# Gelu of the first three tiles from square, exponential and reciprocal on ACT and DVE

## The reference

```python
def _L1_attn_ref(x, A, B, C, gamma, beta):
    uB = jnp.einsum('bld,nd->lbn', x, B)
    def step(state, u_t):
        s = state @ A.T + u_t
        return (s, s)
    _, states = jax.lax.scan(step, init, uB)
    y = jnp.einsum('lbn,dn->bld', states, C)
    act = jax.nn.gelu(y, approximate=False)
    mean = jnp.mean(act, axis=-1, keepdims=True)
    var = jnp.var(act, axis=-1, keepdims=True)
    norm = (act - mean) / jnp.sqrt(var + LN_EPS) * gamma + beta
    return jnp.nan_to_num(norm, nan=0.0, posinf=CLAMP, neginf=-CLAMP)
```

## Time and profile before

| | |
|---|---|
| three runs, us | 1049.47, 1051.88, 1052.98 (median 1051.88) |
| profiled execution, us | 1051.81, its span 1050.0 |
| PE busy | 955.4 us, 91% of the span |
| DVE busy | 630.1 us, 60% |
| ACT busy | 543.5 us, 52% |
| POOL busy | 214.6 us, 20% |
| mean granted clock of PE | 0.977 of full speed |
| loads of ACT's table | 9, of 1.283 us each |

### The profile page before, as it was taken

One profiled execution on the slowest core, in us unless ns is written; L12 is line 12 of the kernel. 1 busy time (PEld: TensorE's weight loads), 2 busy tenths in 40 slices (PEclk: granted clock), 3 DMA queues, 4 the chain that ended last, 5 costly groups with the idle time before them and its releaser, 6 DMA issues.

```text
span 1050.0 us, 35583 instructions
## 1 busy us (share of the span) xinstructions
PE 955.4 (91%) x15476; PEld 630.7 (60%) x15476; DVE 630.1 (60%) x1047; ACT 543.5 (52%) x1020; POOL 214.6 (20%) x246
## 2 busy tenths in 40 slices
PE   5769889999999999999998898898798899999998
PEld 2446565656656666665665565566678544445887
DVE  5745756667485566757767667775653664445421
ACT  4558676676577676466555566567433321212200
POOL 4311112121111211112121121313348410000000
PEclk9989999999999999999999999999799999999999
DMA  8686376462734443454434434323311323232100
GB/s 276 172 285 208 90 214 160 142 178 71 207 93 155 107 121 79 117 124 117 116 100 110 107 101 116 80 66 133 112 50 41 121 83 118 81 105 96 41 1 21
DMA packets 70465, 123.78 MB, mean 118 GB/s; under 512 B 34420, under 2 KB 45716, under 8 KB 67048
## 3 DMA queue, kind: packets, MB, share of 16 engines
q1 hardware_dynamic: 69480, 119.84, 38.9%
q0 software_dynamic: 544, 1.34, 0.4%
q10 hardware_dynamic: 288, 0.33, 0.1%
HBM read 64.81 MB, written 17.31 MB: 78 GB/s over the span
## 4 chain that ended last, share of the span: by engine, by line
PE 66%; DVE 10%; issue 6%; ACT 6%; SPq 4%; DMA 4%; POOL 3%; ACTq 0%; POOLq 0%; DVEq 0%
PE ps L679 65%; SPq L445 4%; DVE mpart L1307 4%; POOL xg L621 3%; ACT p L1082 2%; DMA stage<-in_wkv 1%; DVE rinv L1324 1%; DMA c32b<-in_ctxT 1%; ACT ch L1040 1%; PE ps L818 1%; ACT k L1056 1%; ACT kh L1057 1%; PE ps L848 1%; DVE cl L1282 1%; DMA stage<-in_fw 1%
## 5 line engine op out<-in xcount | busy, mean ns | idle before, releaser
L1307 DVE TENSOR_REDUCE mpart<-ps 128x2 f32<-128x800 f32 (+1 forms) x256 | 252.6, 988 | 131.7 <-PE ps L679 130.8
L1082 ACT ACTIVATE p<-ps 128x512 f32<-128x512 f32 (+1 forms) x416 | 225.4, 595 | 187.7 <-PE ps L679 186.5
L609 POOL TENSOR_TENSOR kl<-k,kh 128x400 f16<-128x400 f32 (+1 forms) x128 | 117.5, 918 | 468.0 <-ACT kh L1057 468.0
L679 PE MATMUL ps<-p,v 128*17 128x64 f32 x6656 | 132.9, 224 | 0.0
L679 PEld LDWEIGHTS ps<-p,v 128*17 128x17 f32 x6656 | 99.5, 99 | 37.4 <-issue 35.5
L679 PE MATMUL ps<-wvh,ch 128*128 128x256 f16 (+1 forms) x416 | 115.1, 277 | 1.7 <-issue 1.7
L679 PE MATMUL ps<-wvh,cl 128*128 128x256 f16 (+1 forms) x416 | 114.3, 275 | 0.0
L679 PE MATMUL ps<-wvl,ch 128*128 128x256 f16 (+1 forms) x416 | 114.3, 275 | 0.0
L679 PE MATMUL ps<-xch,wh 128*128 128x512 f16 (+2 forms) x384 | 114.0, 311 | 0.0
L679 PE MATMUL ps<-xcl,wh 128*128 128x512 f16 (+2 forms) x384 | 113.9, 310 | 0.0
L679 PE MATMUL ps<-xch,wl 128*128 128x512 f16 (+2 forms) x384 | 113.8, 310 | 0.0
(11 more groups left out here) (203 smaller groups left out, 1482.3 us busy)
## 6 DMA issues: line engine op xcount, KB each, us to landing
ks<-kh SPq DMA_DIRECT2D x256, 100.1 KB
w<-in_wgu SPq DMA_DIRECT2D x16, 1024.0 KB, 4.8
ks<-kl SPq DMA_DIRECT2D x128, 100.1 KB
w<-in_wd SPq DMA_DIRECT2D x8, 1024.0 KB, 4.8
c32a<-in_ctxT SPq DMA_DIRECT2D x16, 400.5 KB, 5.2
cparts<-ch SPq DMA_DIRECT2D x8, 800.5 KB, 6.9
cparts<-cl SPq DMA_DIRECT2D x8, 800.5 KB, 9.3
c32a<-in_ctxT SPq DMA_DIRECT2D x12, 400.0 KB, 3.2
```

Of the source, the lines that this page charges most:

```text
L609: nc.gpsimd.tensor_tensor(kl[:, mt, k0:k0 + w], k32[:, ku % 2, 0:w], kh[:, mt, k0:k0 + w], ALU.subtract).then_inc(sem("klo_done"), 1)
L679: return nc.tensor.matmul(o, lhsT, rhs, start=start, stop=stop, skip_group_check=shared)
L1082: nc.scalar.activation(p32[0:n, step % PRING, BANK * side:BANK * side + BANK], ps[0:n, side, :], ACT.Exp, scale=DH ** -0.5).then_inc(sem(" ...
L1307: nc.vector.reduce_max(mpart[:, j0:j0 + 3:2, quarter], o.rearrange("p (b c) -> p b c", b=2)[:, :, 0:w], AX.X).then_inc(sem("max_done"), 1)
```

## The change

For the tiles 0, 1 and 2 the Gelu of `s_y` is replaced by an approximation, `y / (1 + exp(-2a (y + b y^3)))` with a = sqrt(2/pi) and b = 0.044715, which is Gelu's form with a hyperbolic tangent. ACT copies `y` from `mid` to `g_a` and writes its square to `g_m` (step 3). DVE forms `(y^2 + 1/b) y` in `g_z` at its own `s_y` event in step 3, where it had nothing to do before. ACT takes the exponential of it into `g_m` at a new `g_stats` event in step 4. DVE, at `g_stats`, adds one, takes the reciprocal, multiplies by `g_a`, and then takes the statistics as before. Two semaphores are new, `y_cubic` (DVE to ACT) and `y_exp` (ACT to DVE); `gelu` is renamed `y_in`, and is raised after the square. Tile 3 keeps its Gelu.

```diff
--- before.py
+++ after.py
@@ -40,6 +40,8 @@
 F32_MAX = 3.4028234663852886e38
 CLAMP = 1e6
 
+GELU_A, GELU_B = float(np.sqrt(2 / np.pi)), 0.044715
+
 HALVES = [(0, HALF), (HALF, S - HALF)]
 TILE_ROWS = [min(P, S - P * k) for k in range(KT)]
 QUARTERS = [(0, HALF - HALF // 2), (HALF - HALF // 2, HALF // 2), (HALF, HALF // 2), (HALF + HALF // 2, HALF // 2)]
@@ -205,7 +207,7 @@
     return {"out": ("x_added", TT * layer + t + 1), "a_v": ("a_v", t + 1), "a_qk": ("a_qk", t + 1),
             "a_e": ("a_exp", t + 1), "a_w": ("a_wT", t + 1), "a_z": ("a_z", t + 1), "a_x": ("a_added", t + 1),
             "f_gate": ("f_m", t + 1), "q_make": ("q32_done", TT * layer + t + 1), "s_u": ("scan", 7 * t + 1),
-            "s_y": ("gelu", t + 1), "r_logits": ("lgm_in", t + 1), "power": ("am_pow", t + 1)}.get(name)
+            "s_y": ("y_in", t + 1), "r_logits": ("lgm_in", t + 1), "power": ("am_pow", t + 1)}.get(name)
 
 
 def users_before():
@@ -1168,7 +1170,15 @@
                        .then_inc(sem("scan"), 1)
                 elif name == "s_y":
                     act.wait_ge(sem("y_mm"), t + 1)
-                    nc.scalar.activation(g_a[:, :], mid[:, 0:D], ACT.Gelu).then_inc(sem("gelu"), 1)
+                    if t == TT - 1:
+                        nc.scalar.activation(g_a[:, :], mid[:, 0:D], ACT.Gelu).then_inc(sem("y_in"), 1)
+                    else:
+                        nc.scalar.activation(g_a[:, :], mid[:, 0:D], ACT.Copy)
+                        nc.scalar.activation(g_m[:, :], mid[:, 0:D], ACT.Square).then_inc(sem("y_in"), 1)
+                elif name == "g_stats" and t < TT - 1:
+                    act.wait_ge(sem("y_cubic"), t + 1)
+                    nc.scalar.activation(g_m[:, :], g_z[:, :], ACT.Exp, scale=-2 * GELU_A * GELU_B)\
+                       .then_inc(sem("y_exp"), 1)
                 elif name == "r_logits":
                     act.wait_ge(sem("r_top"), t + 1)
                     nc.scalar.activation(pr[:, t:2 * TT:TT, 1:2], prt[:, t:2 * TT:TT, 1:2], ACT.Exp)\
@@ -1473,8 +1483,18 @@
                     nc.vector.tensor_tensor(st_s[:, :, back:NQ], st_s[:, :, back:NQ],
                                             mid[0:N, 0:2 * (NQ - back)].rearrange("n (b q) -> n b q", b=2),
                                             ALU.add).then_inc(sem("scan"), 1)
+                elif name == "s_y" and t < TT - 1:
+                    dve.wait_ge(sem("y_in"), t + 1)
+                    nc.vector.scalar_tensor_tensor(g_z[:, :], g_m[:, :], 1 / GELU_B, g_a[:, :], ALU.add, ALU.mult)\
+                      .then_inc(sem("y_cubic"), 1)
                 elif name == "g_stats":
-                    dve.wait_ge(sem("gelu"), t + 1)
+                    if t < TT - 1:
+                        dve.wait_ge(sem("y_exp"), t + 1)
+                        link(nc.vector.tensor_scalar(g_z[:, :], g_m[:, :], 1.0, None, ALU.add))
+                        link(nc.vector.reciprocal(g_n[:, :], g_z[:, :]))
+                        link(nc.vector.tensor_tensor(g_a[:, :], g_n[:, :], g_a[:, :], ALU.mult))
+                    else:
+                        dve.wait_ge(sem("y_in"), t + 1)
                     stats(g_a[:, :])
                 elif name == "g_norm":
                     link(norm(stats_index(name, layer, t), g_n[:, :], g_a[:, :]))
```

## The result

| | before | after |
|---|---|---|
| runs, us | 1049.46, 1049.47, 1049.96, 1051.88, 1052.98 | 1054.84, 1056.99, 1057.04, 1057.29, 1058.32 |
| median, us | 1049.96 | 1057.04 |
| ratio of after to before | | 1.0058, 95% interval 1.0038 to 1.0079 |
| profiled execution, us (span) | 1051.81 (1050.0) | 1057.29 (1055.5) |
| PE, DVE, ACT busy, us | 955.4, 630.1, 543.5 | 958.4, 638.1, 537.4 |

The changed kernel is slower by 0.58%, about 6 us, though ACT has 6 us less to do. (The means of the runs lie 6.1 us apart, the medians 7.1.) In the profiled executions the spans differ by 5.5 us. In the changed kernel's code the helper lines stand two to ten lines lower (the matmul helper is L681, the maximum L1317, the copy `kh` L1059).

What follows compares the result with a forecast made beforehand. PE waits on ACT's table loads, with DVE next in line; DVE's new row then delays rounds 11, 13 and 15 by 0.90 + 2.25 + 1.15 = 4.3 us, so 1051.8 + 4.3 = 1056.1 us, own range 1053.7 to 1057.8, overall 1050.5 to 1060.5.

Steps and rivals of the forecast that it cites:

- What bounds the kernel: Rounds 11 and 13: PE's K unit waits 1.74 us for ACT's table loads; without them DVE is next in line.
- ACT: Rounds 11, 13, 15: six loads, 7.7 us, go; no cost waiting for y_cubic, O starts earlier, no drain shows.
- The row: Add, reciprocal and multiply on DVE ahead of g_a's statistics take 2.53 us, 1.71 of it the reciprocal.
- Where it lies: Rounds 11, 13: 3.28 us ahead of V6 delay P7's maximum, +0.90 and +2.25 us; round 15's token split, +1.15.
- the last section: Signs of being right: no loads in the rounds, K5 without a wait, P7 waiting 3 to 4 us for mpart.
- The differences per round: Added time of +0.90 us in round 11, +2.25 in round 13 and +1.15 in round 15.
- the pair that was set to cancel: Rounds 11 and 13: 0.2 us less each from DVE's collisions with POOL, 0.2 more from P7 at half rate.
- From this maximum on DVE is the bound: Rounds 11 and 13: DVE rules the stretch from P7's maximum, so the delay there stays to the end.
- The stall decides: Rival: DVE's row hides; rounds 11, 13 and 15 gain 2.4, 1.0 and 1.0 us, giving 1047.4; chance 13%.
- The clock isn't hidden: Rival: idle PE falls to 1.2 GHz in rounds 11 and 13, 1.55 us more each, about 1060; chance 11%.
- The collisions go: Rival: POOL's subtracts miss DVE's work, two held instructions fewer per round, -2.3 us, giving 1053.8; chance 21%.
- The tables stay: Rival: Square needs its own table, six loads stay with DVE's row behind them, giving 1061; chance 3%.

Runs made afterwards that it cites:

- e1: Kernel before, with the Gelu of the first three tiles replaced by a plain copy, so six table loads go and DVE gets nothing more: 1050.31 us, ratio 0.9990.
- e3: Changed kernel without the reciprocal, all hand-overs kept: 1050.81 us, ratio 0.9996 to the kernel before.
- e4: Changed kernel with 33 unneeded matmuls put into PE's wait ahead of P7 in rounds 11 and 13: 1059.35 us, ratio 1.0090 to the kernel before.
- e11: Changed kernel run and profiled again, unchanged: 1058.15 us, ratio 1.0062 to the kernel before.
- e2: Kernel before with Gelu and its loads kept, plus add, reciprocal and multiply ahead of DVE's statistics, result unused: 1058.44 us, ratio 1.0071.
- e10: Changed kernel with Tanh, g_stats behind P6's maximum, and g_clean and all following it one step later (tiles 0, 1): 1046.31 us, ratio 0.9952 to kernel before.
- e6: Changed kernel with Tanh in place of the exponential, without add and reciprocal on DVE: 1051.17 us, ratio 0.9986 to the kernel before.
- e8: Changed kernel, but tile 2 (round 15) keeps its Gelu and two table loads: 1057.33 us, ratio 1.0050 to the kernel before.

## Why the prediction was right

**Forecast.** +0.41% and 1056.1 us stood against +0.58% (0.38 to 0.79) and 1057.04, so the side and the size were right, the size a little small. Part of the closeness of the 1056.1 is luck: it was built on a profiled execution of 1051.8 us, above the 1049.96 that is the median of the five runs before. On 1049.96 the same 4.3 us would have given 1054.3, 2.8 below what was measured.

**What bounds the kernel.** Right. That DVE is next in line was read from round 12's wait of 0.79 us, and e1 confirms it: with the loads gone, P7 waits for DVE.

**ACT.** Right in all points: no load left in the rounds, no wait for `y_cubic`, O earlier, K5 without a wait. The drain that the Trainium skill (ScalarE: Activation LUTs, What ACT_TABLE_LOAD costs) puts at 1.38 us does not show in the changed kernel's tail either: its Gelu starts at 778.17, its load ran from 776.88 to 778.16.

**The row.** 2.53 predicted, 2.56 measured, which is the sum of its terms without the overlap that I took off; the reciprocal took 1.754 us where 1.71 was taken, between the two bounds of 1.68 and 1.90. e3 shows that it carries the loss.

**Where it lies.** V6 at 6.88 predicted, 6.92 measured, P7 at 8.24 and 8.30. P7's maximum came at 8.85 and not at 8.63, as P7 ran at half rate, for which 0.2 had been set aside. The wait is 4.12 us, "almost 4" and outside the "3 to 4" of the last section.

**The differences per round.** 0.90, 2.25 and 1.15 predicted, 0.99, 2.52 and 1.27 measured. Each was measured 10 to 12% larger than predicted. In round 13 0.22 us of the 0.27 are there at P7's maximum (8.85 for 8.63, 0.16 of it from P7 at half rate). In the terms of the sum the term mis-sized is the pair that was set to cancel. P8's maximum started 0.62 us behind the end of DVE's work, since PE ran at 1.2 GHz through K6, which I had called covered (in e4, at the full clock, it started without a wait); and the two held instructions of the kernel before (0.98 and 1.00 us) became one of 1.10. So -0.5 and +0.8 in place of -0.2 and +0.2. "From this maximum on DVE is the bound" holds within these terms: the spare time that PE had ahead of P10, 1.41 us before, shrank to 0.69. Of round 15's 1.15, 1.11 were there at the token split, where the count was made.

**The rivals.** *The stall decides* was mis-sized: it left the 0.75 us of statistics out of P7's time, and would give 3.4 us and not 4.4, by e1. *The clock isn't hidden* came true in its first half, the fall in both rounds; e4 shows why it cost some 0.2 and not 1.55 a round in that profile. *The collisions go* half: one less in each round. *The tables stay* is out.

**What is not settled.** The ratio says 6 us and the rounds' stretches say 4.8 (3.8 in e11). The 4.8 lies inside the interval of 4.0 to 8.3 us; the 3.8 lies below e11's own, 4.5 to 8.6. One candidate lies in the kernel before: in its only profile the clock fell in round 11 and not in round 13, at the same wait, and that made round 11 longer by 1.53 us (23.70 against 22.17). If in most executions it doesn't fall there, the stretches before are 1.5 us shorter and the change costs 6.3 by the stretches (5.3 by e11); the prediction would then have had to say 2.25 for round 11 too, 5.65 in all. No run here shows how often it falls: the kernel before was profiled once. The prediction saw that round 11's clock had fallen, but took this one execution's fall as given.

## What to carry to other kernels

Before you take work off an engine, ask which engine the waiter would wait for next, and look for a place in the same trace where the first wait is missing already: round 12 showed DVE's wait of 0.79 us, and e2 that in rounds 11 and 13 taking out the loads was worth nothing once 2.56 us stood ahead of the maximum. A long instruction on an engine that is nowhere near full (60%) costs its whole length where something urgent is queued behind it and nothing else holds that up (e3: 1.78 to 2.41 us a round for a reciprocal of 1.754; but the row of 2.56 us cost only 0.21 in round 11 of e2, where ACT's wait and the lower clock covered it); first make it short (Tanh instead of Exp and reciprocal, 0.46 us for 2.56), then put it behind what others wait for. And when a rearrangement gains, find the wait that went, since in e10 it was another one than planned.

## What the runs showed of the hardware

A reciprocal on DVE took 0.951 us for 128 elements a partition (read from PSUM), 1.754 for 256 and 3.354 for 512, so 6.25 ns an element, four times a multiply (0.42 for 256). Exp and Tanh share a table here: no load between them. PE's clock fell to 1.2 GHz behind waits of 1.74 us (round 11 before, not round 13) and 1.99 us (round 13 of e1, but not its round 11 and neither round of e4), behind P7's waits of 2.33 us in e3 and 2.00 in e6 in both rounds, and behind the wait of 4.12 us in both rounds of all three executions that had it (after, e8, e11); in e4, where PE worked through all but 0.41 us of the same time, it did not. A DVE instruction that met POOL's subtract of 0.9 us took some 0.6 us longer: 0.87 for 0.29 (multiply of 128x128), 0.89 for 0.28 (`g_f`), 0.99 for 0.43 (the last addition), 1.10 for 0.45 (`copy_predicated`).
